# A selective-scan stage in which TensorE's small turns, gate projections and output projections stand in other steps

## The chip, the cores and the metric

The kernel runs on one core of a Trainium2 chip. The metric is device time in microseconds (us) for one execution of the whole program, median of several runs. The engines are TensorE (PE in the profile, PEld for its weight loads), VectorE (DVE), ScalarE (ACT), GpSimd (POOL) and SyncE (SP), which here issues the DMA transfers.

## What is computed

The program is four transformer-like layers. The change touches one part only, the attention of layer 2, a selective scan over 2 sequences of 1024 tokens with 2048 channels and 16 states. Cut to what matters:

```python
proj = hidden_states @ in_proj_w            # x and z
xc = silu(conv(x));  ssm_p = xc @ x_proj_w.T
dt = softplus(rmsnorm(ssm_p[:R]) @ dt_proj_w.T + dt_bias)
A = -exp(A_log)                             # channel x state
# for each token t, channel d and state n:
h = exp(dt * A) * h + dt * B * x
y = sum_n(h * C)
out = ((y + D_param * xc) * silu(z)) @ out_proj_w.T
```

The work of the scan is therefore, for each of 16 states, one exponential, one product dt\*x\*B, one running recurrence along the tokens, one product with C, and a sum over the states; beside it stand the projections for dt and z and the output projection.

## The kernel before

The function `l2_scan` walks 64 **items**. An item is 128 channels by 512 tokens; 16 items (all channels, `CT`) make a **chunk** of 512 tokens, and there are 4 chunks, 0 to 3. Chunks 0 and 2 begin a sequence (`first(q)`), 1 and 3 take over a carry. Each item has 8 **steps** g = 0 to 7 of two states each, so there are 512 steps in all. Every engine has its own loop over the steps, written out by hand in order, and semaphores tie them together; an engine works strictly down its own list. In this text T, SP and so on are short names for calls:

- VectorE, the recurrence: per step two scans (L3064). In even steps (kind "Y") it also does the product with C (L3075); in odd steps GpSimd does that (L3015). After step 3 comes `pre_c`, after step 4 `pre_dt` (they make dt of the next item), in odd items of chunks 1 to 3 then `proj.add` (L2547), and after step 6 `finish` of the item before (L3038, L3041).
- ScalarE: per step two exponentials (L2943), then at given steps `keep_dtx` (L2911), `gate` (two table loads around a SiLU, L2898 and L2899; the wait for z stands on the SiLU, behind the first load), `keep` (copies the finished sum out of PSUM, L2892), `split` and `log1p` for the next item's dt, and once a chunk `diagonals` (L2923, 16 instructions). The exponentials of steps made by GpSimd go to a PSUM ring of 5 banks, and each waits for the step that used its bank before.
- GpSimd: the product dt\*x\*B (`make_dBx`, L2990) for six of the eight steps, three steps ahead; the product with C in odd steps (L3015); `low` (L2970) and `dtx_` (L2978) for the next item.
- TensorE: in steps 3 and 7 it makes dt\*x\*B itself (`spread`, **SP3** and **SP7**, L2817, 16 matmuls), which is issued in the loop's steps 2 and 6. VectorE's scans of steps 3 and 7 wait for it. `total` (**T0** to **T7**, L2784, 8 transposes) adds a step's product to the sum `yT`; it runs two steps late, T7 right after T6 in step 0 of the next item. T0 clears the sum, so it waits until `keep` has copied the last one. `turn_back` (**TB**, L2827) turns the finished sum back; it waits for dt of the next-but-one item (`dt_ok`), since both use the PSUM tile `small`. `turn_dtx` (**D**, L2806) turns dt\*x for SP3 and SP7, and `keep_dtx` copies it out; `dt_tile` (L2755) makes the raw dt of the next item and waits for `keep_dtx`. `z_part` (L2766) is the projection for z, 8 matmuls of 512 columns an item, and `out_part` (L2536) is the output projection of the chunk before, 8 **pieces** of two such matmuls in every two items of chunks 1 to 3. z and output share one PSUM bank, `big`, so each waits for the gate or the add of the other.
- SyncE: all loads, in one list; `OutProj` loads pieces through a ring of 3.

A **pair** is an even item and the odd one after it; with the output projections the order of the work repeats pair by pair. `SHARE` says how many pieces go into each of the six steps that hold an `out_part`.

## Time and profile before

| | |
|---|---|
| median of 3 runs | 5514.66 us (5511.01 to 5519.32) |
| the profiled execution, its own time | 5513.62 us |
| its span, first to last instruction | 5511.8 us |
| VectorE busy over the span | 3167.7 us (57%) |
| GpSimd busy | 2174.6 us (39%) |
| ScalarE busy | 1970.0 us (36%) |
| TensorE busy | 4853.6 us (88%) |
| the scan, from its first to its last GpSimd or VectorE work | about 2375 to 4413 us of the span |

The scan is a bit over a third of the span. Inside it the shares are quite different from those of the whole: in the 510 us from 3390 to 3900 VectorE is busy 416, GpSimd 422, TensorE 450 and ScalarE 283 us. So no share names the limit. What ends each wait of the engine that carries the recurrence, VectorE, does, and the times in square brackets of a timeline row give just that: the idle time before an instruction, and who ended it. TensorE rows that follow each other share their pipeline, so the start of the next row minus its own start is what the work really takes when nothing is idle between them.

### The profile page before, as it was taken

To read this page: it belongs to the slowest core of one execution; us is meant where nothing else is said; L and a number is where in the kernel's file an instruction comes from. 1 tells how busy PE (TensorE), PEld (TensorE's weight loads), DVE (VectorE), ACT (ScalarE), POOL (GpSimd) and SP (SyncE) were. 2 spreads that over 40 slices of the span, in tenths; PEclk is the share of its full clock that TensorE was granted. 3 is DMA by queue.
4 is the path that set the end of the run, shared out by engine and by line. 5 is a ranking of instruction groups with operands and counts; after the bars stand their busy time and mean duration, and the time that the engine had idled before them with its cause. 6 is when DMAs were issued, how large, how long until landed. Compare 5 with 4: busy or idle time off the path is not lost. (4 is left out here: it accounts for less than half of the span.)

```text
span 5511.8 us, 50241 instructions
## 1 busy us (share of the span) xinstructions
PE 4853.6 (88%) x19120; PEld 2732.7 (50%) x19120; DVE 3167.7 (57%) x3418; ACT 1970.0 (36%) x2873; POOL 2174.6 (39%) x1187
## 2 busy tenths in 40 slices
PE   8997999999778999957778888888888899999998
PEld 4443234477445344435555555555555534467343
DVE  1764478666456133258888887888888822203422
ACT  1563610155232111146565555555555411002100
POOL 1004410000212000059988887888888743100421
PEclk8998999999889999978889999999999999999999
DMA  2001120000010121141133435343643330000101
GB/s 73 1 1 65 46 99 35 31 1 1 8 33 1 61 80 64 45 114 37 41 101 120 128 113 163 115 127 113 172 128 109 105 128 0 23 0 1 47 16 46
DMA packets 177485, 357.26 MB, mean 65 GB/s; under 512 B 21279, under 2 KB 56223, under 8 KB 173151
## 3 DMA queue, kind: packets, MB, share of 16 engines
q1 hardware_dynamic: 169182, 326.26, 19.6%
q0 software_dynamic: 8064, 27.80, 1.3%
q8 instruction: 153, 2.51, 0.2%
q14 instruction: 86, 0.70, 0.0%
HBM read 296.31 MB, written 57.67 MB: 64 GB/s over the span
## 5 line engine op out<-in xcount | busy, mean ns | idle before, releaser
L2990 POOL TENSOR_TENSOR l2scan_h<-l2scan_dtx,l2scan_Bb 128x1024 f32<-128x1024 f32 x384 | 902.4, 2360 | 152.5 <-PE l2scan_yT L2784 139.8
L2943 ACT ACTIVATE l2scan_ring<-l2scan_dt,l2scan_A 128x512 f32<-128x512 f32 x768 | 509.6, 685 | 829.0 <-DVE l2scan_h L3075 446.5
L3015 POOL TENSOR_TENSOR l2scan_h<-l2scan_h,l2scan_Cb 128x1024 f32<-128x1024 f32 x256 | 603.5, 2357 | 94.7 <-DVE l2scan_h L3064 84.4
L2784 PEld LDWEIGHTS l2scan_yT<-ident,l2scan_h 128*128 128x128 f32 x4096 | 505.4, 149 | 243.1 <-issue 160.1
L2784 PE MATMUL l2scan_yT<-ident,l2scan_h 128*128 128x128 f32 x4096 | 558.7, 287 | 56.6 <-POOL l2scan_h L3015 47.8
L2766 PE MATMUL l2scan_big<-state,l2scan_Wz 128*128 128x512 f32 x1024 | 512.3, 635 | 53.5 <-ACT l2scan_zs L2898 29.3
L2411 PE MATMUL l2in_acc<-state,l2in_W 128*128 128x512 f32 x1024 | 444.9, 595 | 10.5 <-DMA l2in_W<-l_attn_in_x 10.5
L2536 PE MATMUL l2scan_big<-l2scan_oy,l2scan_oW 128*128 128x512 f32 x768 | 360.4, 602 | 23.9 <-DMA l2scan_oy<-l_y 11.8
L2766 PEld LDWEIGHTS l2scan_big<-state,l2scan_Wz 128*128 128x128 f32 x1024 | 196.6, 208 | 256.9 <-issue 231.8
L2411 PEld LDWEIGHTS l2in_acc<-state,l2in_W 128*128 128x128 f32 x1024 | 194.4, 190 | 258.7 <-issue 247.4
L3075 DVE TENSOR_TENSOR l2scan_h<-l2scan_ring,l2scan_Cb 128x1024 f32<-128x1024 f32 (+1 forms) x307 | 315.6, 1042 | 4.4
L3064 DVE TENSOR_TENSOR_SCAN l2scan_ring<-l2scan_ring,l2scan_carry,l2scan_h 128x512 f32<-128x512 f32 x256 | 313.0, 1268 | 0.0
L3064 DVE TENSOR_TENSOR_SCAN l2scan_ring<-l2scan_ring,l2scan_h 128x512 f32<-128x512 f32 x256 | 297.4, 1207 | 8.7 <-ACT l2scan_ring L2943 8.7
L2817 PE MATMUL l2scan_ring<-l2scan_dg,l2scan_dtxT 128*128 128x128 f32 x2048 | 249.9, 275 | 0.7 <-DVE l2scan_h L3064 0.7
L3064 DVE TENSOR_TENSOR_SCAN l2scan_h<-l2scan_h,l2scan_carry,l2scan_ring 128x512 f32<-128x512 f32 x128 | 156.8, 1266 | 162.9 <-PE l2scan_ring L2817 162.9
L2467 DVE TENSOR_SCALAR l2in_cv<-l2in_xp,l2in_cw,l2in_cb 128x2048 f32<-128x2048 f32 (+1 forms) x17 | 21.8, 1284 | 397.5 <-ACT l2in_xc L2431 354.4
L3064 DVE TENSOR_TENSOR_SCAN l2scan_h<-l2scan_h,l2scan_ring 128x512 f32<-128x512 f32 x128 | 149.1, 1207 | 157.2 <-PE l2scan_ring L2817 157.2
L2817 PEld LDWEIGHTS l2scan_ring<-l2scan_dg,l2scan_dtxT 128*128 128x128 f32 x2048 | 238.8, 192 | 0.9 <-DVE l2scan_h L3064 0.9
L2198 PE MATMUL l3pair_bank<-state,l3ffn_W 128*128 128x512 f32 x512 | 225.6, 593 | 0.0
L3204 PE MATMUL l2pair_bank<-state,l2ffn_W 128*128 128x512 f32 x512 | 221.6, 592 | 0.0
L2536 PEld LDWEIGHTS l2scan_big<-l2scan_oy,l2scan_oW 128*128 128x128 f32 x768 | 133.7, 191 | 166.4 <-issue 105.6
L2443 ACT ACTIVATE l2in_xp<-l2in_acc 128x512 f32<-128x512 f32 x64 | 38.2, 597 | 482.6 <-PE l2in_acc L2411 482.6
(424 smaller groups left out, 8407.1 us busy)
## 6 DMA issues: line engine op xcount, KB each, us to landing
l2scan_oy<-l_y SPq DMA_DIRECT2D x192, 512.0 KB, 6.1
l2scan_Wz<-l_attn_in_z SPq DMA_DIRECT2D x64, 512.0 KB, 3.6
l2scan_oW<-l_attn_out_w SPq DMA_DIRECT2D x192, 128.0 KB, 4.2
l_xc<-l2in_xc SPq DMA_DIRECT2D x16, 1024.0 KB, 4.8
l2scan_xc<-l_xc SPq DMA_DIRECT2D x64, 256.0 KB, 5.0
l2scan_Cb<-l_bc SPq DMA_DIRECT2D x128, 128.0 KB, 6.2
l_y<-l2scan_zs SPq DMA_DIRECT2D x64, 256.0 KB, 3.7
l2scan_Bb<-l_bc SPq DMA_DIRECT2D x96, 128.0 KB, 5.2
```

What stands on the lines that cost most here:

```text
L2198: t.matmul(acc, self.W[:, k, m * P:(m + 1) * P], x[:, k, :], start=k == 0, stop=False)
L2411: last = t.matmul(acc[:, n % 4, :], W[:, ct % 2, k, :], x[:, k, :], start=k == 0, stop=k == KT - 1)
L2536: last = t.matmul(self.acc, self.W[:, j, k], self.y[:, j, k], start=kp == 0 and k == 0, stop=kp == PIECES - 1 and k == PIECE - 1)
L2766: last = t.matmul(big[:, :], Wz[:, q % 2, k, :], x[:, k, :], start=k == 0, stop=k == KT - 1)
L2784: last = t.matmul(yT[:, k, :], h[:, st % SLOTS, j, k * P:(k + 1) * P], K.ident[:, :], is_transpose=True, start=g == 0 and j == 0 and k == ...
L2817: last = t.matmul(bank(st, j)[:, k * P:(k + 1) * P], dtxT[:, k, :], dg[:, i, k, :], start=True, stop=True)
L2943: a.activation(bank(st, j) if maker(st) == "P" else h[:, st % SLOTS, j, :], dt[:, q % 2, :], ACT.Exp, scale=A[:, ct, n:n + 1]).then_inc(dA ...
L2990: g_.tensor_tensor(h[:, st % SLOTS], dtx[:, None, :].to_broadcast([P, SGR, NT]), Bb[:, rows_at(g), :], ALU.mult).then_inc(dBx_ok, 1)
L3015: g_.tensor_tensor(hs, hs, Cb[:, g * SGR:(g + 1) * SGR, :], ALU.mult).then_inc(hC_g, 1)
L3064: last = v.tensor_tensor_scan(out, dA, dBx, init, ALU.mult, ALU.add)
L3075: last = v.tensor_tensor(hs[:, js], src, Cb[:, g * SGR + js.start:g * SGR + js.stop, :], ALU.mult)
L3204: last = t.matmul(acc, self.W[:, k, m * P:(m + 1) * P], x[:, k, :], start=k == 0, stop=k == KT - 1)
```

## The change

TensorE's list: TB of the item before moves from step 5 (ahead of T3) to step 6 (behind T4, ahead of SP7). D moves from step 7 of the item before to step 0 of the item itself, between T6 and T7, and once a chunk `turn_rows` moves with it from step 6. The z projection of an even item moves from steps 1, 2, 3 to steps 2, 3, 4 (2, 3 and 3 matmuls), that of an odd item from steps 5, 6, 7 to steps 6, 7 and step 0 of the next item (2, 4, 2). The output pieces move from steps 5 to 10 of a pair to steps 6 to 11, with one piece fewer ahead of the odd item's SP3. The very first item's z moves from steps 1 to 3 to steps 6 to 8. ScalarE's list: `keep_dtx` and `diagonals` move from step 2 to step 1, the first gate from step 6 to step 10. VectorE, GpSimd and SyncE keep their lists. No instruction is added or taken away.

```diff
--- before.py
+++ after.py
@@ -2501,7 +2501,7 @@
 
 
 
-    SHARE = (1, 1, 2, 1, 2, 1)
+    SHARE = (1, 1, 2, 1, 1, 2)
 
     def __init__(self, s, K, w, y_dram, y_out, acc):
         self.K, self.w, self.y_dram, self.y_out, self.acc = K, w, y_dram, y_out, acc
@@ -2833,30 +2833,38 @@
                 for st in range(STEPS):
                     q, g = divmod(st, NSG)
                     s16 = g + NSG * (q % 2)
-                    if g == 5 and q:
-                        turn_back(q - 1)
                     if g != 1 and st >= 2:
                         total(st - 2)
-                    if g == 0 and st:
+                    if g == 0 and q:
+                        if q % CT == 0:
+                            turn_rows(q // CT)
+                        turn_dtx(q)
                         total(st - 1)
+                    if g == 6 and q:
+                        turn_back(q - 1)
                     if st + 1 < STEPS and maker(st + 1) == "T":
                         spread(st + 1)
                     if g == 1 and q + 1 < ITEMS:
                         dt_tile(q + 1)
-                    if g == 6 and q + 1 < ITEMS and (q + 1) % CT == 0:
-                        turn_rows((q + 1) // CT)
-                    if g == 7 and q + 1 < ITEMS:
-                        turn_dtx(q + 1)
-                    if s16 in (1, 13):
-                        z_part(q, 0, 3)
-                    if s16 in (2, 14):
-                        z_part(q, 3, 6)
-                    if s16 in (3, 15):
-                        z_part(q, 6, KT)
-                    if 5 <= s16 < 11 and q >= CT:
-                        out_part(q - q % 2, s16 - 5)
+                    if s16 == 0 and q:
+                        z_part(q - 1, 6, KT)
+                    if st == 6 or q and s16 == 2:
+                        z_part(q, 0, 2)
+                    if st == 7 or q and s16 == 3:
+                        z_part(q, 2, 5)
+                    if st == 8:
+                        z_part(0, 5, KT)
+                    if q and s16 == 4:
+                        z_part(q, 5, KT)
+                    if s16 == 14:
+                        z_part(q, 0, 2)
+                    if s16 == 15:
+                        z_part(q, 2, 6)
+                    if 6 <= s16 < 12 and q >= CT:
+                        out_part(q - q % 2, s16 - 6)
                 total(STEPS - 2)
                 total(STEPS - 1)
+                z_part(ITEMS - 1, 6, KT)
                 turn_back(ITEMS - 1)
 
             @block.scalar
@@ -2943,13 +2951,12 @@
                         a.activation(bank(st, j) if maker(st) == "P" else h[:, st % SLOTS, j, :], dt[:, q % 2, :], ACT.Exp, scale=A[:, ct, n:n + 1]).then_inc(dA_ok, 1)
                     if g == 0 and q and ct == 0:
                         columns(c)
-                    if g == 2:
-                        if q:
-                            keep_dtx(q)
-                        if q and ct == 0:
+                    if g == 1 and q:
+                        keep_dtx(q)
+                        if ct == 0:
                             diagonals(c)
-                        if q and q % 2 == 0:
-                            gate(q - 1)
+                    if g == 2 and q and q % 2 == 0:
+                        gate(q - 1)
                     if g == 3:
                         if q:
                             keep(q - 1)
@@ -2957,7 +2964,9 @@
                             split(q + 1)
                     if g == 4 and q + 1 < ITEMS:
                         log1p(q + 1)
-                    if g == 6 and q % 2 == 0:
+                    if st == 10:
+                        gate(0)
+                    if g == 6 and q and q % 2 == 0:
                         gate(q)
                 keep(ITEMS - 1)
                 gate(ITEMS - 1)
```

Three places in the built order. First TensorE, chunks 1 to 3, from SP7 of an even item to SP3 of the odd one (l2scan_yT is a total, l2scan_oy an output piece of two matmuls, l2scan_dtx is D, Wdt is `dt_tile`, l2scan_dg a spread). Before:

```order
L2817 MATMUL l2scan_ring<-l2scan_dg,l2scan_dtxT 128x128 x8
L2536 MATMUL l2scan_big<-l2scan_oy,l2scan_oW 128x512 x2
L2784 MATMUL l2scan_yT<-ident,l2scan_h 128x128 x8
L2806 MATMUL l2scan_small<-ident,l2scan_dtx 128x128 x4
L2536 MATMUL l2scan_big<-l2scan_oy,l2scan_oW 128x512 x4
L2784 MATMUL l2scan_yT<-ident,l2scan_h 128x128 x16
L2536 MATMUL l2scan_big<-l2scan_oy,l2scan_oW 128x512 x2
L2755 MATMUL l2scan_small<-l2scan_ssm,l2scan_Wdt 128x512
L2536 MATMUL l2scan_big<-l2scan_oy,l2scan_oW 128x512 x4
L2784 MATMUL l2scan_yT<-ident,l2scan_h 128x128 x8
L2817 MATMUL l2scan_ring<-l2scan_dg,l2scan_dtxT 128x128 x8
```

Now:

```order
L2817 MATMUL l2scan_ring<-l2scan_dg,l2scan_dtxT 128x128 x8
L2536 MATMUL l2scan_big<-l2scan_oy,l2scan_oW 128x512 x2
L2784 MATMUL l2scan_yT<-ident,l2scan_h 128x128 x8
L2536 MATMUL l2scan_big<-l2scan_oy,l2scan_oW 128x512 x2
L2784 MATMUL l2scan_yT<-ident,l2scan_h 128x128 x8
L2806 MATMUL l2scan_small<-ident,l2scan_dtx 128x128 x4
L2784 MATMUL l2scan_yT<-ident,l2scan_h 128x128 x8
L2536 MATMUL l2scan_big<-l2scan_oy,l2scan_oW 128x512 x4
L2755 MATMUL l2scan_small<-l2scan_ssm,l2scan_Wdt 128x512
L2536 MATMUL l2scan_big<-l2scan_oy,l2scan_oW 128x512 x2
L2784 MATMUL l2scan_yT<-ident,l2scan_h 128x128 x8
L2817 MATMUL l2scan_ring<-l2scan_dg,l2scan_dtxT 128x128 x8
```

D has moved between T6 and T7, six pieces between the two spreads have become five, and three of these now stand behind T7.

Second TensorE, the odd item of the same pair, from SP3 to SP7 (l2scan_ysb is TB, l2scan_Wz the z projection). Before:

```order
L2817 MATMUL l2scan_ring<-l2scan_dg,l2scan_dtxT 128x128 x8
L2536 MATMUL l2scan_big<-l2scan_oy,l2scan_oW 128x512 x2
L2784 MATMUL l2scan_yT<-ident,l2scan_h 128x128 x16
L2827 MATMUL l2scan_small<-ident,l2scan_ysb 128x128 x4
L2784 MATMUL l2scan_yT<-ident,l2scan_h 128x128 x8
L2766 MATMUL l2scan_big<-state,l2scan_Wz 128x512 x3
L2784 MATMUL l2scan_yT<-ident,l2scan_h 128x128 x8
L2817 MATMUL l2scan_ring<-l2scan_dg,l2scan_dtxT 128x128 x8
```

Now:

```order
L2817 MATMUL l2scan_ring<-l2scan_dg,l2scan_dtxT 128x128 x8
L2536 MATMUL l2scan_big<-l2scan_oy,l2scan_oW 128x512 x2
L2784 MATMUL l2scan_yT<-ident,l2scan_h 128x128 x8
L2536 MATMUL l2scan_big<-l2scan_oy,l2scan_oW 128x512 x4
L2784 MATMUL l2scan_yT<-ident,l2scan_h 128x128 x24
L2827 MATMUL l2scan_small<-ident,l2scan_ysb 128x128 x4
L2817 MATMUL l2scan_ring<-l2scan_dg,l2scan_dtxT 128x128 x8
```

TB has gone behind T3 and T4, directly ahead of SP7, and the three z matmuls ahead of SP7 have gone behind it.

Third ScalarE, the even item, from the exponentials of steps 0 to 2 to `keep` (l2scan_dtxT is `keep_dtx`, l2scan_zs the SiLU of the gate, l2scan_ysb `keep`). Before:

```order
L2943 ACTIVATE l2scan_ring<-l2scan_dt,l2scan_A 128x512 x6
L2911 ACTIVATE l2scan_dtxT<-l2scan_small 128x512
L2898 ACT_TABLE_LOAD
L2898 ACTIVATE l2scan_zs<-l2scan_big 128x512
L2899 ACT_TABLE_LOAD
L2943 ACTIVATE l2scan_h<-l2scan_dt,l2scan_A 128x512 x2
L2892 ACTIVATE l2scan_ysb<-l2scan_yT 128x512
```

Now (the lines of the changed file are 8 higher):

```order
L2951 ACTIVATE l2scan_ring<-l2scan_dt,l2scan_A 128x512 x4
L2919 ACTIVATE l2scan_dtxT<-l2scan_small 128x512
L2951 ACTIVATE l2scan_ring<-l2scan_dt,l2scan_A 128x512 x2
L2906 ACT_TABLE_LOAD
L2906 ACTIVATE l2scan_zs<-l2scan_big 128x512
L2907 ACT_TABLE_LOAD
L2951 ACTIVATE l2scan_h<-l2scan_dt,l2scan_A 128x512 x2
L2900 ACTIVATE l2scan_ysb<-l2scan_yT 128x512
```

`keep_dtx` has gone ahead of step 2's exponentials; the gate and `keep` stand where they stood.

## Rows read from the trace of the kernel before

**Rows 1.** VectorE's waits, chunk 0, then chunks 1-3: us in total, times, longest.
```profile
DVE l2scan_h L3064 <- PE l2scan_ring L2817: 47.6, 23, 3.5
...
DVE l2scan_h L3064 <- PE l2scan_ring L2817: 253.9, 71, 10.5
```

**Rows 2.** VectorE timeline, scans that waited: start, us, what ran, [idle before <-releaser].
```profile
2919.64 2.45 DVE L3064 TENSOR_TENSOR_SCAN l2scan_h<-l2scan_h,l2scan_carry,l2scan_ring 128x512 f32<-128x512 f32 x2 [5.17 <-PE l2scan_ring L2817]
...
2936.61 2.45 DVE L3064 TENSOR_TENSOR_SCAN l2scan_h<-l2scan_h,l2scan_carry,l2scan_ring 128x512 f32<-128x512 f32 x2 [1.68 <-PE l2scan_ring L2817]
...
3206.13 2.45 DVE L3064 TENSOR_TENSOR_SCAN l2scan_h<-l2scan_h,l2scan_carry,l2scan_ring 128x512 f32<-128x512 f32 x2 [3.33 <-PE l2scan_ring L2817]
...
3237.31 2.45 DVE L3064 TENSOR_TENSOR_SCAN l2scan_h<-l2scan_h,l2scan_carry,l2scan_ring 128x512 f32<-128x512 f32 x2 [4.53 <-PE l2scan_ring L2817]
...
3254.17 2.45 DVE L3064 TENSOR_TENSOR_SCAN l2scan_h<-l2scan_h,l2scan_carry,l2scan_ring 128x512 f32<-128x512 f32 x2 [1.57 <-PE l2scan_ring L2817]
...
3269.55 2.45 DVE L3064 TENSOR_TENSOR_SCAN l2scan_h<-l2scan_h,l2scan_carry,l2scan_ring 128x512 f32<-128x512 f32 x2 [3.33 <-PE l2scan_ring L2817]
...
4342.78 2.45 DVE L3064 TENSOR_TENSOR_SCAN l2scan_h<-l2scan_h,l2scan_carry,l2scan_ring 128x512 f32<-128x512 f32 x2 [1.87 <-PE l2scan_ring L2817]
...
4389.37 2.45 DVE L3064 TENSOR_TENSOR_SCAN l2scan_h<-l2scan_h,l2scan_carry,l2scan_ring 128x512 f32<-128x512 f32 x2 [4.56 <-PE l2scan_ring L2817]
```

**Rows 3.** ScalarE timeline, an even item's steps 2 and 3.
```profile
3260.27 0.69 ACT L2943 ACTIVATE l2scan_ring<-l2scan_dt,l2scan_A 128x512 f32<-128x512 f32 x1 [2.31 <-DVE l2scan_h L3075]
3260.90 0.58 ACT L2911 ACTIVATE l2scan_dtxT<-l2scan_small 128x512 f32<-128x512 f32 x1
3261.50 1.28 ACT L2898 ACT_TABLE_LOAD   x1
...
3265.94 0.57 ACT L2892 ACTIVATE l2scan_ysb<-l2scan_yT 128x512 f32<-128x512 f32 x1
```

**Rows 4.** TensorE timeline, an odd item and the next even one.
```profile
3226.49 1.91 PE L2784 MATMUL l2scan_yT<-ident,l2scan_h 128*128 128x128 f32 x16
...
3235.32 1.95 PE L2817 MATMUL l2scan_ring<-l2scan_dg,l2scan_dtxT 128*128 128x128 f32 x16
...
3244.68 1.09 PE L2827 MATMUL l2scan_small<-ident,l2scan_ysb 128*128 128x128 f32 x4 [3.94 <-issue]
...
3247.26 4.21 PE L2766 MATMUL l2scan_big<-state,l2scan_Wz 128*128 128x512 f32 x6
...
3263.53 2.81 PE L2766 MATMUL l2scan_big<-state,l2scan_Wz 128*128 128x512 f32 x6 [0.81 <-ACT l2scan_zs L2898]
```

**Rows 5.** Windows there: us, PE busy (x), granted clock, DMA share, GB/s.
```profile
3240.00:3241.00 1.00, 0.74 (x7) 1.00 0.00 0
...
3247.00:3248.00 1.00, 1.00 (x4) 0.50 0.07 16
```

**Rows 6.** GpSimd timeline, step 7 of that pair's even item.
```profile
3224.17 2.35 POOL L3015 TENSOR_TENSOR l2scan_h<-l2scan_h,l2scan_Cb 128x1024 f32<-128x1024 f32 x1
```

**Rows 7.** Timelines of the first item: TensorE, VectorE, GpSimd.
```profile
2403.34 4.70 PE L2766 MATMUL l2scan_big<-state,l2scan_Wz 128*128 128x512 f32 x6 [23.45 <-DMA l2scan_Wz<-l_attn_in_z]
...
2410.74 2.33 DVE L3064 TENSOR_TENSOR_SCAN l2scan_h<-l2scan_h,l2scan_ring 128x512 f32<-128x512 f32 x2 [18.58 <-PE l2scan_ring L2817]
...
2393.30 2.34 POOL L2990 TENSOR_TENSOR l2scan_h<-l2scan_dtx,l2scan_Bb 128x1024 f32<-128x1024 f32 x1
```

**Rows 8.** TensorE timeline in chunk 0, what ran after idle time.
```profile
2483.93 1.09 PE L2784 MATMUL l2scan_yT<-ident,l2scan_h 128*128 128x128 f32 x8 [2.15 <-POOL l2scan_h L3015]
...
2666.77 1.97 PE L2784 MATMUL l2scan_yT<-ident,l2scan_h 128*128 128x128 f32 x8 [3.11 <-POOL l2scan_h L3015]
2668.53 1.73 PE L2755 MATMUL l2scan_small<-l2scan_ssm,l2scan_Wdt 128*128 128x512 f32 x2
```

**Rows 9.** ScalarE and VectorE timelines at the start of chunk 1.
```profile
2872.80 4.77 ACT L2923 ACTIVATE l2scan_dg<-ident,l2scan_BT 128x128 f32<-128x128 f32 x16
...
2887.80 2.45 DVE L3064 TENSOR_TENSOR_SCAN l2scan_h<-l2scan_h,l2scan_carry,l2scan_ring 128x512 f32<-128x512 f32 x2 [10.16 <-PE l2scan_ring L2817]
```

## The prediction

> **What bounds the kernel now.** I read the waits of VectorE first, since the recurrence runs there and every other engine works a few steps ahead of it or behind it. One cause makes nearly all of its idle time: the spreads that TensorE owes to the scans of steps 3 and 7. They cost 47.6 us in chunk 0 behind the first item and 253.9 us in chunks 1 to 3 [rows 1], and 18.58 us once in the first item [rows 7]: 320 us in all, the most that the change can win. No engine is full; TensorE is late because it stands in waits of its own ahead of the spreads.
>
> The VectorE timeline splits this by place. Call the start of an even item's third-step scan A, of the odd item's third-step scan B, of the odd item's seventh-step scan C. One pair reads A 3206.13, B 3237.31, C 3254.17, next A 3269.55, with waits of 4.53 before B, 1.57 before C, 3.33 before A [rows 2]. VectorE's own work is then 31.18 - 4.53 = 26.65 from A to B, 15.3 from B to C, 12.05 from C to A; and 26.65 - 12.05 = 14.6 from A to the even item's seventh step, which never waits. Over chunks 1 to 3 the 24 waits before B sum to 128.1 (first 5.17, last 4.56), the 23 before C to 26.0 (first 1.68, last 1.87), and 21 before A are 3.3 to 3.5 each; three more, at the starts of chunks, are about 10 [rows 2, 9]. In chunk 0 the same three kinds sum to 10, 12 and 25.
>
> **The start.** TensorE stood 23.45 us for the first z weights with SP3 of item 0 behind it [rows 7]. Now z of item 0 comes in step 6, by when the weights have landed (2403). T0 and SP3 follow the product of step 0 and, at the low clock, end about when VectorE has finished step 2, so the 18.6 us go. What is late next: GpSimd has one more product to make (its last before the stop started at 2393.3 [rows 7]; 2.3), then step 3's product with C (2.35), then `low` (1.3), and `pre_dt` waits for that, some 3 us. I take **-15** (-10 to -18).
>
> **TB behind T4.** Before C TensorE stood 3.94 us at TB for dt, and what followed ran slow: TB took 1.09, three z matmuls 4.21 where the next three took 2.81 [rows 4]. The granted clock says why: 1.00 (2.4 GHz) while it still worked, 0.50 (1.2 GHz) after the idle time [rows 5]. Now T2, T3, T4 and two more pieces stand ahead of TB. From SP3 to SP7 TensorE has 4 totals (0.9 each, half of the 1.91 row), 3 pieces (1.9 each, from 2.81 for three such matmuls), TB and a spread (1.95) [rows 4]: 11.5 us, against 15.3 that VectorE needs. dt is there 7.4 us after B (3244.68 less 3237.31 [rows 2, 4]), when TB's turn comes after four totals and three pieces, 9 us, so TB doesn't wait. C then doesn't wait: **-26** in chunks 1 to 3, **-12** in chunk 0. The cover is almost 4 us. In the even item the same sum with eight z matmuls is 13.6 against 14.6: covered still, by 1 us.
>
> **One piece fewer before B.** What releases T7 is GpSimd's product of step 7; in this pair it ends at 3224.17 + 2.35 = 3226.52, 20.4 after A [rows 6]. GpSimd works on the same list without gaps up to there, so this doesn't move. Now D, T5, T6 and two pieces are done ahead of it, and behind it come T7, two pieces, `dt_tile`, one piece, T0, SP3. Before, T6, T7 and the same work took 3226.49 to 3237.31, 10.8 us [rows 2, 4]; without T6 that is 9.9. B comes 20.4 + 9.9 = 30.3 after A, a wait of 3.7 against a mean of 128.1/24 = 5.3: -1.6 a pair, -39 in all, at full clock. But TensorE now idles about 2.2 us ahead of T7. The nearest rows are in chunk 0: after 2.15 us idle T took 1.09, almost full speed; after 3.11 idle T and `dt_tile` took 1.97 and 1.73, some 1.5 more than at full speed [rows 8]. I take 0.75, the middle: **-21** (-39 to +3). In chunk 0 there are no pieces and GpSimd rules before and after: 0.
>
> **A.** The chain to A runs through ScalarE: exponential, `keep_dtx`, gate, two exponentials, `keep`, then T0 and SP3 on TensorE [rows 3]. Moving `keep_dtx` a step forward takes its 0.6 us out (3260.90 to 3261.50). The gate must not wait in its place. z of the odd item is ready only in the next item now: T7 starts 20.4 - 15.3 = 5.1 after C, then T7 and two matmuls, 7.9 after C. The SiLU wants it at 6.1 (exponential) + 0.63 + 1.28 (table load) = 8.0 [rows 3]. That is a margin of 0.1 us. Further, nothing stands on TensorE between `dt_tile` (done 8.9 after C) and T0 (11.7 after C, when `keep` is done); z stood there before. An idle time of 2.9 us lies next to the 3.11 one, which cost 1.5, and above the 2.15 one, which cost nothing [rows 8]; I take 1.0. So A changes by +0.35, over 21 + 7 pairs **+10** (-17 to +57, the last if T0 and SP3 run wholly at the low clock, +2.65).
>
> The Trainium skill, page "TensorE: Matmul & The Clock Gate", section "Why this matters for your kernels", advises against idle gaps between bursts of matmuls, as the clock then falls back to half. By that rule the gap ahead of T0 would be paid in full, +57 in place of +10, for a total of about 5495, and with the gap ahead of T7 it is the last rival below; by rows 8 such gaps are paid in part, and the sum stays with the rows.
>
> **Starts of chunks.** `diagonals` (4.77 us [rows 9]) leaves the chain between step 2 and `keep`, but now delays step 2's exponentials, since `turn_rows` and D come late. By the same steps A comes 20 to 22.5 after C; it was 22.1 (12 own and 10.16 wait [rows 9]). **-3** (-6 to +1). The end of the scan has two z matmuls more ahead of the last TB: **+1**.
>
> **Sum:** -15 - 26 - 12 - 21 + 10 - 3 + 1 = -66. The profiled execution took 5513.6 us, 1 below the median of 5514.7, so the median goes to **5448 us**. My own range for this case is 5425 to 5475.
>
> **Rivals.** (1) **The clock holds.** The gaps of 2.2 and 2.9 us cost nothing: -18 at B, -28 at A more, hence 5514 - 112 = about **5401**. For it: the row after 2.15 us. Against: the one after 3.11 [rows 8]. (2) **z late.** T7, two z matmuls and the SiLU have 0.1 us to spare. If the clock is low there, or GpSimd late, the gate waits some 1.2 us in each of 28 pairs: +34, **5482**. (3) **Only the start.** The waits swap places (T7, T0 and the clock give back what TB gave): -15, **5500**. (4) **Slower: the clock falls at both gaps in every pair.** Then A loses 2.65 - 0.6 = 2.0 in 28 pairs, +57, and B, with T7, two pieces and `dt_tile` at half speed, loses about as much as the slow stretch behind TB had to lose (0.46 + 1.4 + a slow total, 2.7) less 1.6, +26 in 24 pairs. With -15 - 38 - 2 + 1 that is +29: **5544**. It decides against the change from a mean loss of about 3.7 us a pair, since all gains together are some 114 us over 31 pairs. For it: the change creates both gaps, where before useful work stood. Against: the idle time at TB, longer than either, goes.
>
> **How the numbers follow.** Forecast 0.46, clock holds 0.18, z late 0.18, only the start 0.10, slower 0.08. The range 5400 to 5500 takes in the forecast, nearly all of the second and third and half of the fourth. A measurement of this kernel can tell 0.2%, 11 us, from no change: faster by more 0.86 (all but the last two and a part of the fourth), within 0.05, slower by more 0.09.
>
> **What would show it.** The first SP3 scan without its 18.6 us, T7's and C's waits: none before C, 3.5 to 4.5 before B, about 3.7 before A. GpSimd's step-7 product still 20.4 after A. TensorE idle ahead of T7 and T0 with the granted clock between 1.00 and 0.50. The prediction is wrong if C still waits, if the SiLU idles for z, if the wait before A is over 5, or if GpSimd comes to wait for totals.

## The result and the profile after

The changed kernel takes 5494.11 us (median of 15 runs, 5485.65 to 5512.31) against 5514.66 for the kernel before: ratio 0.9965, 95% interval 0.9956 to 0.9974, or 20 us less. The forecast was 5448, 66 us less. The direction was right; of the size less than a third came.

The two profiled executions differ by only 10 us (5503.46 against 5513.62), and that number misleads. The stages ahead of the scan, whose code is the same, stand 17 us apart. The first `dt_tile` of the scan in the kernel before (TensorE timeline: start, us, what ran, idle time and its releaser):

```profile
2366.57 2.08 PE L2755 MATMUL l2scan_small<-l2scan_ssm,l2scan_Wdt 128*128 128x512 f32 x2 [20.98 <-DMA l2scan_Wdt<-l_attn_dt_proj]
```

The same instruction in the changed kernel:

```profile
2383.59 2.07 PE L2755 MATMUL l2scan_small<-l2scan_ssm,l2scan_Wdt 128*128 128x512 f32 x2 [20.78 <-DMA l2scan_Wdt<-l_attn_dt_proj]
```

So I compare the scan alone, from the start of its first scan instruction to the start of its last: 2020.8 us before, 1993.0 after, 27.8 less. Over the 16 kernels profiled in this study, all with these same stages ahead, the scan's first instruction starts anywhere from 2381.3 to 2399.6.

VectorE's waits for the spreads in the changed kernel, chunk 0 behind the first item, then chunks 1 to 3 (us in total, times, longest), against 47.6 and 253.9 before [rows 1]:

```profile
DVE l2scan_h L3073 <- PE l2scan_ring L2817: 59.1, 15, 10.6
...
DVE l2scan_h L3073 <- PE l2scan_ring L2817: 221.7, 48, 7.8
DVE l2scan_ring L3073 <- ACT l2scan_ring L2951: 10.4, 3, 3.9
```

Chunk 0 waits more than before, chunks 1 to 3 less, and a wait for exponentials is new, once at the start of each later chunk. One pair in the VectorE timeline shows where: A, B, C and the next A.

```profile
3085.91 2.45 DVE L3073 TENSOR_TENSOR_SCAN l2scan_h<-l2scan_h,l2scan_carry,l2scan_ring 128x512 f32<-128x512 f32 x2 [5.32 <-PE l2scan_ring L2817]
...
3116.11 2.45 DVE L3073 TENSOR_TENSOR_SCAN l2scan_h<-l2scan_h,l2scan_carry,l2scan_ring 128x512 f32<-128x512 f32 x2 [3.54 <-PE l2scan_ring L2817]
...
3131.25 2.44 DVE L3073 TENSOR_TENSOR_SCAN l2scan_h<-l2scan_h,l2scan_carry,l2scan_ring 128x512 f32<-128x512 f32 x2
...
3147.51 2.45 DVE L3073 TENSOR_TENSOR_SCAN l2scan_h<-l2scan_h,l2scan_carry,l2scan_ring 128x512 f32<-128x512 f32 x2 [4.15 <-PE l2scan_ring L2817]
```

C no longer waits (1.57 in [rows 2]). B waits 3.54, where it waited 4.53. A waits 5.32 and 4.15, where it waited 3.33. TensorE ahead of the first of these A scans:

```profile
3073.77 1.09 PE L2784 MATMUL l2scan_yT<-ident,l2scan_h 128*128 128x128 f32 x8 [1.12 <-POOL l2scan_h L3024]
...
3076.41 1.02 PE L2755 MATMUL l2scan_small<-l2scan_ssm,l2scan_Wdt 128*128 128x512 f32 x2
...
3080.51 1.94 PE L2784 MATMUL l2scan_yT<-ident,l2scan_h 128*128 128x128 f32 x8 [3.08 <-ACT l2scan_ysb L2900]
...
3082.24 3.62 PE L2817 MATMUL l2scan_ring<-l2scan_dg,l2scan_dtxT 128*128 128x128 f32 x16
```

ScalarE beside it:

```profile
3074.64 0.69 ACT L2951 ACTIVATE l2scan_ring<-l2scan_dt,l2scan_A 128x512 f32<-128x512 f32 x1 [0.77 <-DVE l2scan_h L3084]
...
3075.35 1.28 ACT L2906 ACT_TABLE_LOAD   x1
...
3079.79 0.57 ACT L2900 ACTIVATE l2scan_ysb<-l2scan_yT 128x512 f32<-128x512 f32 x1
```

TensorE has nothing between `dt_tile` and T0 for 3.08 us; T0 waits for `keep`, which on ScalarE stands behind the gate (3075.35) and step 3's exponentials. T0 then takes 1.94 and SP3 3.62 us, where T takes 1.04 and SP3 1.95 at full speed. The windows there (us, PE busy, granted clock, DMA share, GB/s) have the clock at 1.00 in the idle time and at 0.50, 1.2 GHz, in the work behind it:

```profile
3078.00:3079.00 1.00, 0.00 (x0) 1.00 0.75 295
...
3080.00:3081.00 1.00, 0.49 (x3) 0.50 0.78 187
...
3084.00:3085.00 1.00, 1.00 (x6) 0.50 1.07 399
```

Ahead of T7 the idle time is shorter, and here the clock held:

```profile
3106.30 1.09 PE L2784 MATMUL l2scan_yT<-ident,l2scan_h 128*128 128x128 f32 x8 [1.83 <-POOL l2scan_h L3024]
...
3107.23 3.60 PE L2536 MATMUL l2scan_big<-l2scan_oy,l2scan_oW 128*128 128x512 f32 x8
```

The second item is the one place that I had not looked at. B of item 1 waits 10.58 us (2.27 before), in the VectorE timeline:

```profile
2449.39 2.33 DVE L3073 TENSOR_TENSOR_SCAN l2scan_h<-l2scan_h,l2scan_ring 128x512 f32<-128x512 f32 x2 [10.58 <-PE l2scan_ring L2817]
```

On TensorE `dt_tile` waited for its weights:

```profile
2443.07 2.07 PE L2755 MATMUL l2scan_small<-l2scan_ssm,l2scan_Wdt 128*128 128x512 f32 x2 [4.41 <-DMA l2scan_Wdt<-l_attn_dt_proj]
```

And SyncE issued those only when z of item 0 was done, behind the z weights that wait for it:

```profile
2438.69 0.33 SPq L2657 DMA_DIRECT2D l2scan_Wz<-l_attn_in_z  x1
...
2439.53 0.43 SPq L2663 DMA_DIRECT2D l2scan_Wdt<-l_attn_dt_proj  x1
```

### The profile page after: what moved, and what is told of

It reads as the page before. It is cut to its first block and busy times, and to the rows that moved or that the text cites. A ratio compares the mean times of both kernels' runs of the same rounds, so it can differ in the third digit from the quotient of the medians.

```text
span 5501.7 us, 50241 instructions
## 1 busy us (share of the span) xinstructions
PE 4859.0 (88%) x19120; PEld 2759.0 (50%) x19120; DVE 3165.5 (58%) x3418; ACT 1972.9 (36%) x2873; POOL 2175.9 (40%) x1187
## 5 line engine op out<-in xcount | busy, mean ns | idle before, releaser
L2766 PE MATMUL l2scan_big<-state,l2scan_Wz 128*128 128x512 f32 x1024 | 476.8, 598 | 0.0
L2817 PE MATMUL l2scan_ring<-l2scan_dg,l2scan_dtxT 128*128 128x128 f32 x2048 | 284.8, 296 | 5.4 <-DVE l2scan_h L3073 5.2
L2817 PEld LDWEIGHTS l2scan_ring<-l2scan_dg,l2scan_dtxT 128*128 128x128 f32 x2048 | 271.7, 213 | 9.2 <-DVE l2scan_h L3073 9.2
L2766 PEld LDWEIGHTS l2scan_big<-state,l2scan_Wz 128*128 128x128 f32 x1024 | 182.4, 194 | 157.0 <-issue 157.0
```

The lines of the kernel that those rows point to most:

```text
L2766: last = t.matmul(big[:, :], Wz[:, q % 2, k, :], x[:, k, :], start=k == 0, stop=k == KT - 1)
L2817: last = t.matmul(bank(st, j)[:, k * P:(k + 1) * P], dtxT[:, k, :], dg[:, i, k, :], start=True, stop=True)
```

## The experiments

All times stand against the kernel before, run beside them on the same chip. The scan's length and the waits of VectorE are added from the timeline rows of each profile: A over 21 pairs of chunks 1 to 3 (without each chunk's first), B over all 24, C over all 24 with any wait of `finish` just ahead of it.

| kernel | median us | ratio [95%] | scan us | A | B | C |
|---|---|---|---|---|---|---|
| before | 5514.7 | | 2020.8 | 70.7 | 128.1 | 26.0 |
| changed | 5494.1 | 0.9965 [0.9956, 0.9974] | 1993.0 | 97.7 | 102.7 | 0 |
| e5 before + TB moved | 5533.5 | 1.0036 [1.0019, 1.0053] | 2041.1 | 70.7 | 139.9 | 21.4 |
| e13 before + TB, D moved | 5603.4 | 1.0154 [1.0116, 1.0192] | 2096.3 | 105.9 | 123.7 | 20.4 |
| e12 before + projections moved | 5518.8 | 1.0002 [0.9986, 1.0019] | 2014.6 | 108.1 | 112.5 | 0 |
| e9 changed, TB back | 5504.2 | 0.9976 [0.9966, 0.9987] | 1994.4 | 94.2 | 101.0 | 0 |
| e6 before + start moved | 5516.5 | 0.9997 [0.9985, 1.0009] | 2017.4 | 70.8 | 130.5 | 24.2 |
| e1 changed, gap ahead of T0 filled | 5475.3 | 0.9912 [0.9893, 0.9931] | 1969.5 | 65.3 | 113.4 | 0 |
| e3 changed, work ahead of T7 | 5462.0 | 0.9901 [0.9880, 0.9923] | 1964.9 | 96.4 | 78.0 | 0 |
| e11 changed, both gaps | 5439.0 | 0.9854 [0.9830, 0.9878] | 1936.1 | 65.3 | 79.7 | 0 |
| e2 changed, `keep` first | 5411.6 | 0.9797 [0.9777, 0.9817] | 1908.8 | 3.5 | 107.3 | 0 |
| e8 before, `keep` first | 5523.5 | 1.0008 [0.9996, 1.0020] | 2026.4 | 74.4 | 127.4 | 23.0 |
| e10 e2 + dt weights first | 5396.5 | 0.9780 [0.9757, 0.9803] | 1899.2 | 3.6 | 111.3 | 0 |
| e7 e10 + pieces moved | 5324.2 | 0.9649 [0.9629, 0.9669] | 1823.2 | 0 | 9.4 | 0 |
| e4 changed, SyncE's order | 5485.0 | 0.9941 [0.9923, 0.9960] | 1991.2 | 94.6 | 102.6 | 0 |
| e14 e7, first gate later | 5323.5 | 0.9646 [0.9621, 0.9671] | 1818.5 | 0.2 | 9.6 | 0 |

### Which part of the change did it

The turn back alone, in the kernel before:

```diff
-                    if g == 5 and q:
-                        turn_back(q - 1)
                     if g != 1 and st >= 2:
                         total(st - 2)
+                    if g == 6 and q:
+                        turn_back(q - 1)
```

> The kernel before, with only the turn back moved from step 5 to step 6, behind T4. If the prediction's terms for it stand alone, C no longer waits (1.1 us a pair in 24 pairs of chunks 1 to 3, 26 us, and 13 us in chunk 0), A and B keep their waits of 3.3 and 5.3 us, and the time is 5514 - 39 = 5476 (5470 to 5483). Rival: the time given back at C is taken at the next place (A's T0 waits for keep on ScalarE, whose time does not move with C): then A waits up to 1.1 us more and the time is within 10 us of 5514.

It is 20 us longer by the ratio to the runs beside it, not 39 shorter, and A did not wait longer (70.7), so neither figure of the expectation came. TensorE around the turn back:

```profile
3249.20 1.09 PE L2784 MATMUL l2scan_yT<-ident,l2scan_h 128*128 128x128 f32 x8 [1.51 <-POOL l2scan_h L3015]
...
3252.27 5.46 PE L2766 MATMUL l2scan_big<-state,l2scan_Wz 128*128 128x512 f32 x6 [1.98 <-DVE state L2547]
...
3258.86 0.60 PE L2827 MATMUL l2scan_small<-ident,l2scan_ysb 128*128 128x128 f32 x4
```

VectorE's `finish` behind it:

```profile
3259.50 0.76 DVE L3038 SCALAR_TENSOR_TENSOR l2scan_small<-l2scan_xc,l2scan_Dp,l2scan_small 128x512 f32<-128x512 f32 x1 [1.33 <-PE l2scan_small L2827]
```

With the output pieces still in their old steps TensorE runs out of work at T4 and again ahead of z, which waits for `proj.add`. Six passes (three matmuls) take 5.46 us, about twice the 2.81 of [rows 4], and now T4, TB and SP7 all stand behind them, so `finish` waits too. In all the waits before the even item's step 7 come to 18.8 us in chunks 1 to 3, where there were none. In chunk 0, which has no pieces, C's waits do fall, from 13.1 to 2.1. The converse, the turn back alone put back into the changed kernel (the same lines the other way):

> The changed kernel, with only the turn back put back to step 5, ahead of T3 and T4. If the wait at C was the turn back standing ahead of the work that C needs, C waits again, 1.1 us a pair (39 us in all 32 pairs), and the time is 5494 + 39 = 5533. Rival: since the z of the item now starts one step later (the turn back alone, moved in the kernel before, made it 16 us slower, because the z matmuls started late and slow and ended behind finish), the turn back's place no longer matters: C waits under 0.3 us and the time is within 10 us of 5494.

```profile
3185.00 0.63 PE L2827 MATMUL l2scan_small<-ident,l2scan_ysb 128*128 128x128 f32 x4 [0.50 <-issue]
...
3187.21 1.95 PE L2817 MATMUL l2scan_ring<-l2scan_dg,l2scan_dtxT 128*128 128x128 f32 x16
```

C does not wait, though TB stands in its old step: TB now idles 0.50 us instead of the 3.94 of [rows 4], since two pieces stand in the gap, and SP7 runs at full speed. The time is 6 us above the changed kernel's by the ratios, whose intervals overlap, so the turn back's place has no effect here that these runs can tell. Two more runs take the turns and the projections apart. The first moves the projections and the first item's z, as the change does (cut):

```diff
-                    if s16 in (1, 13):
-                        z_part(q, 0, 3)
...
+                    if s16 == 14:
+                        z_part(q, 0, 2)
...
-                    if 5 <= s16 < 11 and q >= CT:
+                    if 6 <= s16 < 12 and q >= CT:
```

> The kernel before, with only the gate and output projections one step later (and the first item's z and gate late): the turn back stays at step 5 and the turn of dt*x at step 7 of the item before. With the turn back alone put back into the changed kernel, C did not wait and the time was 5504; with the turn back alone moved in the kernel before, the time was 5533. Theory (the projections carry the change): C does not wait here either, A waits 4 to 5.3 us, B 3.5 to 5.3, and the time is within 10 us of the changed kernel: 5504 (5494 to 5514). Rival (the parts need each other): the turn of dt*x at step 7 holds SP7's successors or D comes before the z of its item, C waits over 0.5 us and the time is above 5514.

The second has e5's edit and the turn of dt\*x (cut: `keep_dtx` and `diagonals` move with it on ScalarE):

```diff
                     if g == 0 and q:
+                        if q % CT == 0:
+                            turn_rows(q // CT)
+                        turn_dtx(q)
                         total(st - 1)
...
-                    if g == 7 and q + 1 < ITEMS:
-                        turn_dtx(q + 1)
```

> The kernel before, with only the two turns moved (the turn back to step 6 behind T4, the turn of dt*x to the head of its item) and all projections in their old steps. Theory (the projections carry the change): no gain; the z matmuls of odd items still start behind a gap of 3 to 4 us at step 5, at 1.2 GHz, C waits 0.5 to 1 us in chunks 1 to 3, and the time is between the kernel before and the turn back alone: 5517 to 5535. Rival (the turns carry it): 5500 or less.

The projections alone take C's waits away (26.0 to 0) and 16 us of B's, and lose nearly as much, 37, at A (70.7 to 108.1): D then waits for `finish` in step 7, and T0 stands behind the widest gap of all, with the clock down:

```profile
3196.07 0.63 PE L2806 MATMUL l2scan_small<-ident,l2scan_dtx 128*128 128x128 f32 x4 [0.85 <-DVE l2scan_zs L3052]
...
3208.33 1.94 PE L2784 MATMUL l2scan_yT<-ident,l2scan_h 128*128 128x128 f32 x8 [3.57 <-ACT l2scan_ysb L2901]
...
3210.06 3.62 PE L2817 MATMUL l2scan_ring<-l2scan_dg,l2scan_dtxT 128*128 128x128 f32 x16
```

C went as the first theory had it, the time did not. The ratio can't be told from 1: its interval stands for 5507 to 5525 beside 5514.7, which leaves out the theory's 5504 and the changed kernel's 5494, though not the 5514 that was to part theory and rival. So the projections don't carry the change; the gain needs both moves. The turns alone cost 1.5%, far outside both figures of the expectation. In the even item z waits for the SiLU with nothing left ahead of it, now runs slow (4.51 where [rows 4] have 2.81), and T0 and SP3 stand behind it: A loses 35 us. Another 35 go before the even item's step 7, as in e5:

```profile
3158.49 4.51 PE L2766 MATMUL l2scan_big<-state,l2scan_Wz 128*128 128x512 f32 x6 [2.00 <-ACT l2scan_zs L2897]
```

So neither half gives anything alone (+1 and +85 us by the ratios, the first with the first item's move in it), and both together give -20. The first item alone (cut):

```diff
-                    if s16 in (1, 13):
-                        z_part(q, 0, 3)
+                    if st == 6 or s16 == 13 or q and s16 == 1:
+                        z_part(q, 0, 3)
...
+                    if st == 10:
+                        gate(0)
```

> The kernel before, with only the first item's z matmuls in steps 6 to 8 and its gate behind step 10. A of item 0 no longer waits 18.6 us for the z weights. By SyncE's queue the second item pays for it: dt_tile of item 2 waits for its weights and B of item 1 waits about 10 us instead of 2.3, so the gain is 18.6 - 8 - some 3 us at pre_dt = 8: 5506 (5503 to 5510). Rival: the wait of item 1 came from the turns' new places, then the gain is 15 or more: 5499 or less.

The first item's A lost its 18.6 us, B of item 1 waited 10.1, and the scan came 3.4 us shorter; the ratio can't be told from 1, so neither 5506 nor 5499 came.

### The clock in the two gaps

In e1 the gap ahead of T0 is filled with work of no use:

```diff
-                    t.matmul(small[:, :], Wdt[:, q % 2, :], ssm[:, c % 2, :], start=True, stop=True).then_inc(dt_ready, 1)
+                    for _ in range(4 if q % 2 and q > 2 else 1):
+                        last = t.matmul(small[:, :], Wdt[:, q % 2, :], ssm[:, c % 2, :], start=True, stop=True)
+                    last.then_inc(dt_ready, 1)
```

> The changed kernel, with the matmul of dt_tile issued four times instead of once in each even item from item 2 on (same operands, same tile, the signal on the last). Nothing else moves; the three copies take 3 x 0.86 = 2.6 us of the 3.08 us that TensorE idles ahead of T0. Theory 1 (the clock): T0 and SP3 run at 1.2 GHz (1.94 and 3.62 us) because TensorE idled; with the gap filled they take 1.04 and 1.95, A waits 5.3 - 2.6 = 2.7 us, and the 31 pairs give 31 x (1.0 to 2.6): 30 to 80 us less than the changed kernel, 5415 to 5465. Theory 2 (the order on ScalarE): A waits because T0 can't start before keep, and the clock adds little; A waits over 4 us still, and the time is within 10 us of the changed kernel's 5494.

```profile
3063.03 3.60 PE L2756 MATMUL l2scan_small<-l2scan_ssm,l2scan_Wdt 128*128 128x512 f32 x8
...
3067.14 1.06 PE L2786 MATMUL l2scan_yT<-ident,l2scan_h 128*128 128x128 f32 x8 [0.52 <-ACT l2scan_ysb L2902]
...
3068.04 1.95 PE L2819 MATMUL l2scan_ring<-l2scan_dg,l2scan_dtxT 128*128 128x128 f32 x16
...
3090.42 1.35 PE L2786 MATMUL l2scan_yT<-ident,l2scan_h 128*128 128x128 f32 x8 [2.22 <-POOL l2scan_h L3026]
...
3091.57 5.07 PE L2536 MATMUL l2scan_big<-l2scan_oy,l2scan_oW 128*128 128x512 f32 x8
```

T0 and SP3 are at full speed and A waits 2.75 to 2.82 in chunks 1 and 3, the 2.7 of the forecast's own full-clock figure. In chunk 2 it waits 3.67 to 3.84. That is 32 us less at A. But 11 of them went again at B: in 13 of 24 pairs (6 in the changed kernel) B waited some 1.6 us longer than in the others (5.2 for 3.6, in chunk 2 6.1 for 4.5), with the pieces behind T7 at 5.07 instead of 3.60 (last two rows) though the gap ahead of T7 had not changed. The gain was 19 us by the medians, 24 in the scan and 29 by the ratios; 5475 lies above the expected 5415 to 5465.

In e3 work that exists anyway goes ahead of T7 (the even items' last two z matmuls likewise):

```diff
                         turn_dtx(q)
+                        if s16 == 0:
+                            z_part(q - 1, 6, KT)
+                        elif q >= CT:
+                            proj.matmuls(t, proj.pieces((q - CT) // 2, 2)[0])
                         total(st - 1)
...
-                    if s16 == 0 and q:
-                        z_part(q - 1, 6, KT)
```

> The changed kernel, with work that it already has moved into the gap in which TensorE waits for T7's carry product: in odd items the first of the two output pieces of step 8 (1.88 us; the gap is 1.8 to 2.6), in even items the last two z matmuls (1.88 us; the gap is 1.12). Theory 1 (the clock): the pairs in which B waits 5.1 to 6.3 us are those in which the clock fell in the T7 gap; they go to 3.6 or less, and since 1.9 us of pieces no longer stand between T7 and SP3, B's wait falls by up to 1.9 us in all 24 pairs of chunks 1 to 3: 24 x 1.9 = 45 us plus 9 x 2 = 18 for the clock, 5430 to 5450. In even items T7 comes 0.8 us later, keep does not wait for it by as much, so nothing. Rival: the piece overlaps the carry product on the way to SP3, but SP3's end is set elsewhere (step 3's exponentials); then B's wait stays at 3.5 and the time within 10 us of 5494.

B's longer waits are gone and its sum fell by 25, where 45 and 18 for the clock were expected; 5462 lies above the expected 5430 to 5450. `dt_tile` now came to wait for its weights:

```profile
3091.53 1.12 PE L2755 MATMUL l2scan_small<-l2scan_ssm,l2scan_Wdt 128*128 128x512 f32 x2 [1.19 <-DMA l2scan_Wdt<-l_attn_dt_proj]
```

e11 has e1's filler and, in odd items, e3's piece:

> The changed kernel with both of TensorE's gaps filled and ScalarE's order as it is: dt_tile's matmul four times in even items (ahead of T0, A), and one of the two output pieces of step 8 ahead of T7 in odd items (B). With one gap filled alone, A's wait fell from a mean of 4.65 us to 2.8 but B's rose from 4.28 to 4.7, or B's fell to 3.3 and A's stayed at 4.4. If the clock is what made the changed kernel miss its forecast, both fall together: A 2.8 and B 3.3 us, so 21 x 1.85 = 39, 24 x 1.0 = 24 and some 6 us in chunk 0 less: 5425 (5415 to 5440), slightly below the forecast of 5448. Rival: what the gaps cost moves on to a third place (TensorE waits for the carry product in step 1 or 2, or the pieces' weights come late): then the time stays at 5450 or more.

With both gaps filled both sums fall together, and the time is 5439 (5434 by the ratio). That it lies near the forecast is a coincidence: the forecast had already paid 28 us at A and 18 at B for the clock, and its figure for a clock that holds is rival (1)'s 5401. What the clock cost the changed kernel is 32 us at A in chunks 1 to 3, 6 in chunk 0, and some 10 at B, the six pairs of 24 that waited 1.6 to 1.8 longer. e11 gives 23 at B, so about 13 of these are the piece's better place. The 30 and more us that e11 stays above 5401 are not the clock in these gaps; the last part of the text says where most of them lie.

### What holds A

```diff
                     if g == 2 and q and q % 2 == 0:
+                        keep(q - 1)
                         gate(q - 1)
                     if g == 3:
-                        if q:
+                        if q % 2:
                             keep(q - 1)
```

> The changed kernel, with keep of the odd item ahead of its gate on ScalarE (in step 2 of the even item) instead of behind it and step 3's two exponentials. In the changed kernel keep starts 5.1 us after T7 of the odd item ends (3074.70 to 3079.79), and T0 waits for it. Theory 2 (the order on ScalarE holds A): T0 follows dt_tile without a gap, at 3077.3 instead of 3080.5, SP3 ends at about 3080.1 instead of 3085.9, and A's wait of 4.0 to 5.3 us falls below 1: 31 pairs x 4 = 120 us less, 5375, if nothing else is next; if step 3's exponentials (then at about 3079.2 to 3080.5) or the z matmuls come next, half of it, 5435. Theory 1 (the clock): the gap is gone too, so the gain is at least the 1.0 to 2.6 us a pair of the run that fills the gap. A rival: the exponential behind the gate comes 0.6 us later and A waits for that; then 5480 or more.

A's wait is gone altogether in chunks 1 and 3 behind their first pairs, and 0.4 to 0.6 in chunk 2, without a filler. T0 follows at once behind `dt_tile` and finds the clock up:

```profile
3044.97 1.04 PE L2784 MATMUL l2scan_yT<-ident,l2scan_h 128*128 128x128 f32 x8
...
3045.84 1.95 PE L2817 MATMUL l2scan_ring<-l2scan_dg,l2scan_dtxT 128*128 128x128 f32 x16
```

So e1 cured a symptom (the clock, 1.3 to 2.5 us) and e2 the cause (`keep` behind gate and exponentials, all of it). The same edit in the kernel before:

> The kernel before, with only keep of the odd item ahead of its gate. In the kernel before, too, T0 of the even item waits for keep, and keep stands behind the gate and two exponentials (3198.07 to 3202.52), but z matmuls stand ahead of T0 as well and wait for the gate's SiLU (3200.11). If ScalarE's order alone sets A there, A's wait of 3.3 us goes in 30 pairs: 5514 - 100 = 5414. If the z matmuls, which wait for the SiLU and take 2.8 us, hold T0 as much, the wait stays at 2.5 or more and the time above 5490; then the change to the projections was needed for the gain of the run with keep ahead of the gate in the changed kernel.

Nothing: A waits 3.4 to 3.8, no less than before. The z matmuls stand ahead of T0 there and wait for the SiLU [rows 4]. The change opened a way that the kernel before didn't have, and did not use it.

On top of e2, SyncE's list in e10:

```diff
                     late = ()
+                    if q + 2 < ITEMS:
+                        dt_weights(q + 2)
...
                         channels(q + 2)
-                        dt_weights(q + 2)
```

> The changed kernel with keep ahead of the gate (5412 in its own run) and the dt weights issued at the head of each item, without the move of the output pieces. Expected: the first items of chunks 2 and 3 lose their waits of 8.1 and 10.4 us down to about 2, item 1 waits 2 us less (it still waits for the z of item 0), B keeps 3.5 to 5.3 us: 5412 - 16 = 5396 (5390 to 5405). Then the rest of the difference to 5324 is the move of the output pieces. Rival: the dt weights were late by the same amount in every pair and hid it in B's wait; then B falls below 3.5 here too and the time is under 5380.

As expected: the first A scans of chunks 2 and 3 wait 2.9 and 1.4 instead of 8.1 and 10.4, B stays. Then the output pieces:

```diff
-    SHARE = (1, 1, 2, 1, 1, 2)
+    SHARE = (1, 1, 2, 0, 2, 2)
...
                         turn_dtx(q)
+                        if q % 2 and q >= CT:
+                            proj.matmuls(t, proj.pieces((q - CT) // 2, 2)[0])
                         total(st - 1)
...
-                        out_part(q - q % 2, s16 - 6)
+                        if s16 == 8:
+                            proj.matmuls(t, proj.pieces((q - CT) // 2, 2)[1])
+                        else:
+                            out_part(q - q % 2, s16 - 6)
```

> The changed kernel with three edits: keep of the odd item ahead of its gate (which took A's wait away and gave 5412 in its own run); in odd items one output piece of step 8 in the gap ahead of T7 and the pieces of step 9 moved behind SP3 (SHARE 1, 1, 2, 0, 2, 2), so that one piece stands between T7 and SP3 instead of three; and the dt weights issued at the head of each item in SyncE's queue, since with work in the T7 gap dt_tile waited 1.2 us for them. Theory (TensorE's work between T7 and SP3 sets B): SP3 ends 1.9 + 1.9 us earlier and B's wait falls from 3.5 to 5.3 us to below 1; 24 pairs x 3.5 = 85 us, the first items of chunks 2 and 3 no longer wait for dt weights (5 us each) and item 1 8 us: 5412 - 100 = 5312 (5300 to 5330). Rival: the carry product on GpSimd or step 3's exponentials come next and hold B; then 5370 or more.

```profile
DVE l2scan_small L3044 <- ACT l2scan_small L2898: 27.2, 23, 1.7
DVE state L2547 <- PE l2scan_big L2536: 17.0, 24, 1.6
DVE l2scan_h L3081 <- PE l2scan_ring L2819: 11.2, 13, 1.8
```

B's 111.3 fell to 9.4; those rows of VectorE's waits in chunks 1 to 3 are what is left. A pair takes 56.0 us in them, where VectorE's own work is 54. This kernel is 3.5% faster than the one before and 170 us faster than the changed one.

### The second item

```diff
-                    if q % 2 == 0 and q + 2 < ITEMS:
+                    if q and q % 2 == 0 and q + 2 < ITEMS:
                         z_weights(q + 2)
...
+                    if q == 0:
+                        z_weights(2)
```

> The changed kernel, with one DMA issue of SyncE moved: the z weights of item 2, which wait for the z of item 0, stand behind the channels and dt weights of item 2 instead of ahead of them. Theory (SyncE's queue): B of item 1 waits 10.6 us in the changed kernel because dt_tile of item 2 waits 4.4 us for its weights, which stand behind the wait for the later z; with them ahead it waits about 2.3 us as in the kernel before, and A of item 2 comes 8 us earlier: 5486 (5483 to 5490). Rival: the 10.6 us come from the z matmuls of item 0 themselves, which now lie in steps 6 to 8 ahead of SP3; then B still waits 8 or more and the time stays at 5494.

The wait for the weights went, B's wait did not (9.73): ScalarE's SiLU waits 4.47 us for the late z with `keep` behind it, and T0 waits for that. My theory of SyncE's queue falls, though the time, 5485 in four runs, lies inside the range that the theory had given (5483 to 5490): the scan came only 1.8 us shorter than the changed kernel's, and B still waits, so the time does not speak for the theory. ScalarE, then TensorE:

```profile
2421.45 0.60 ACT L2908 ACTIVATE l2scan_zs<-l2scan_big 128x512 f32<-128x512 f32 x1 [4.47 <-PE l2scan_big L2768]
```

```profile
2425.31 1.07 PE L2786 MATMUL l2scan_yT<-ident,l2scan_h 128*128 128x128 f32 x8 [3.05 <-ACT l2scan_ysb L2902]
```

```diff
                             split(q + 1)
+                    if st == 11:
+                        gate(0)
...
-                    if st == 10:
-                        gate(0)
```

> The kernel with the three edits (5324 in its own run), with the first item's gate behind keep and split of step 11 instead of step 10. With the dt weights in time, B of item 1 still waited 8.3 to 9.9 us. Theory: it is the same wait as at A, the gate ahead of keep on ScalarE (its SiLU waits 4.5 us for the late z and keep stands behind it); with the gate behind keep, B of item 1 waits 1 to 2.5 us and the time falls by 6 to 8: 5317 (5310 to 5322). Rival: the z matmuls of item 0 on TensorE themselves hold T0 and SP3 of item 1 (2.7 to 4.4 us in step 8): then B waits 5 or more and the time stays within 3 us of 5324.

B of item 1 now waits 5.0 instead of 8.3, between the two theories: the gate's place held 3.3 of it. In its trace T7 (1.97) and three z matmuls (3.52) still stand, slow, ahead of T0. The time did not move measurably (5323.5 against 5324.2).

## Why the prediction was off

In the order of its terms, with what the traces of before and after measure:

| term | forecast | measured | from |
|---|---|---|---|
| start | -15 | -5 | 18.6 gone; 8.3 new before B of item 1, 5.1 before `pre_dt` |
| C | -38 | -39 | 26.0 and 13.1 us of waits, now none |
| B | -21 | -21 | 128.1 to 102.7 in chunks 1 to 3; 7.8 to 12.2 in chunk 0 |
| A | +10 | +39 | 70.7 to 97.7; 24.4 to 36.3 in chunk 0 |
| starts of chunks | -3 | +3 | A 29.1 to 21.4, but 10.4 for exponentials |
| end | +1 | +1 | `finish` 5.0 to 5.8 |
| sum | -66 | -23 | the scan: -28 |

Some 5 us of the scan's difference stand in no row; 2.4 of them are shorter waits of `pre_dt` in later items.

**A is the step that failed**, 29 of the 43 us between the two sums. The idle time itself was named and forecast well, 2.9 us against 3.08. Two sizes in the term were wrong, and e1, in which the clock ahead of T0 holds, parts them.

The larger one is late z, rival (2), which the forecast put at nothing by a margin of 0.1 us. At full clock A was to wait 0.6 less in 28 pairs, -17. In e1 the same sum is +1 (70.7 to 65.3 in chunks 1 to 3, 24.4 to 30.4 in chunk 0). Nearly all of these 18 us lie in chunks 0 and 2. There the gate waited for z in all 14 pairs behind the first ones, 1.1 us in chunk 0 and 0.7 to 0.9 in chunk 2; in chunks 1 and 3 it never did, and A's full-clock wait of 2.75 to 2.82 is the forecast's 2.7. C, T7, the z matmuls and the SiLU in chunk 0, with GpSimd's rows ahead of T7:

```profile
2463.71 2.32 DVE L3073 TENSOR_TENSOR_SCAN l2scan_h<-l2scan_h,l2scan_ring 128x512 f32<-128x512 f32 x2
...
2467.55 0.18 POOL L3022 COPY l2scan_carry<-l2scan_h 128x2 f32<-128x2 f32 x1
2467.81 2.36 POOL L3024 TENSOR_TENSOR l2scan_h<-l2scan_h,l2scan_Cb 128x1024 f32<-128x1024 f32 x1
...
2470.22 1.09 PE L2784 MATMUL l2scan_yT<-ident,l2scan_h 128*128 128x128 f32 x8 [1.36 <-POOL l2scan_h L3024]
2471.15 1.88 PE L2766 MATMUL l2scan_big<-state,l2scan_Wz 128*128 128x512 f32 x4
...
2473.07 0.60 ACT L2906 ACTIVATE l2scan_zs<-l2scan_big 128x512 f32<-128x512 f32 x1 [1.08 <-PE l2scan_big L2766]
```

The clock is not the reason, T7 and z run at full speed. T7 starts 6.5 us after C here and 5.9 in chunk 2, against 5.1 forecast and 5.2 in chunks 1 and 3. The forecast had read its times in one pair of chunk 1 and used them in all chunks. In these two chunks, each of which begins a sequence, GpSimd also copies the carry ahead of its product, and VectorE's own work is shorter (26.0 us from A to B for 26.65). That this is what makes z late is read from the rows; no run tests it.

The other 10 us are the price of the clock. I took 1.0 us a pair, 28 in all, between two rows of chunk 0 [rows 8]; e1 against the changed kernel gives 32 us in chunks 1 to 3 and 6 in chunk 0, 1.4 a pair. Pair by pair A lost nothing in 6 of 28, 1.2 to 1.7 in 15 and 2.5 in 7, always with the same T and SP3 behind 3.05 to 3.15 us of idle time. SP3 alone can lose 1.7 (3.62 for 1.95).

The Trainium skill, page "TensorE: Matmul & The Clock Gate", section "Why this matters for your kernels", would have had the gap ahead of T0 paid in full, and "about 5495" stood in the prediction for it. The measured time is 5494. The trace agrees that such a gap costs: in 18 of 21 pairs of chunks 1 to 3 A waited longer than e1's full-clock values. But that the numbers agree is luck. Paid in full, 2.65 us in 28 pairs are 74 us; 38 were measured, nearer the 28 that the rows had given, and the rest of A's +39 came from late z.

Rival (3), 5500, lies nearest of the others, and half of it came true: A lost what C gained. But B kept its gain, and of the start's 15 us a third came.

**The start** was mis-sized. The 18.6 us went, as said, and `pre_dt` waited 5.1 for the forecast 3; that ScalarE's first gate, TensorE's z and SyncE's `z_weights(2)` would all land in item 1 was not seen, though the rule of counting every queue that a step is moved past would have found it: 8.3 us at B of item 1. e4 and e14 show that SyncE's order is not what holds B there, and that the gate's place is 3.3 us of it (8.3 to 5.0); the rest stays open.

**C** came out right in size (its waits in chunk 0 sum to 13.1, not the 12 that was read) and, for chunks 1 to 3, wrong in cause, so the match is luck. The prediction put it on the turn back's place; e5 shows that this alone gives no time in chunks 1 to 3, and e9 and e12 that C's waits go with the projections, whether TB stands in step 5 or 6. Its sum counted TensorE's work from SP3 to SP7 with everything moved at once, so it could not tell the two apart.

**B** has the forecast's sum, but by misses that cancel. At full clock it waits 3.54 to 3.60 in chunks 1 and 3 against 3.7, and 4.5 to 4.6 in chunk 2, where VectorE comes sooner and T7 later: some 8 us more. The clock cost 10 us where 18 were taken, and chunk 0, put at 0, lost 4.

**Starts of chunks**: `diagonals` did delay step 2's exponentials, and VectorE waited 3.2 to 3.9 us for them at each start, more than the chain to `keep` gave back.

Of the list of signs, A over 5 us came true in 9 of the 21 pairs, and the SiLU idled for z in chunks 0 and 2: two of the four signs set against the forecast. The other two did not come: C does not wait, and GpSimd waits less for totals than before (80 us for 140). T7 still starts 20.4 after A (3106.30 less 3085.91).

## What to carry to other kernels

Before pricing a move on the engine that seems late, follow its wait back through the other engines' lists: here T0 waited for a copy on ScalarE that stood behind a gate with two table loads, and putting the copy first gave 83 us where the whole change gave 20, though only once the change had taken z out of the way (e8). Check a thin margin in every kind of stretch that it must hold in: here 0.1 us, read in one pair, held in chunks 1 and 3 and failed in 0 and 2. The work behind an idle gap on TensorE bounds what the clock can cost, 2.5 us here, and work that is there anyway can fill the gap: e3's two moves gained 32 us by the medians, 28 in the scan. Test parts of a move in both directions (alone, and undone in the whole), because here each half alone was worth nothing or cost 1.5%, and only the pair gained.
